# Two sorting networks of a four-layer graph network kernel: VectorE's steps ordered by drains instead of a semaphore

## The chip, the cores and the metric

The kernel runs on one core of a Trainium2 chip. The metric is the device time of one execution in microseconds (us), the median of several runs; less is better.

## What is computed

The reference is four graph layers on 3,125 nodes of 64 features and 53,125 edges (two directions of 25,000 random edges and a loop per node). Each layer normalises the nodes, gathers rows along the edges, reduces them per node and adds the result. Cut to what matters here:

```python
edge_index = jnp.stack([src, dst])
h = relu(layernorm(x)); x = x + L0(h, edge_index, edge_attr_32, ...)     # segment sum, max, mean by src
h = relu(layernorm(x)); x = x + L1(h, edge_index, ...)                   # attention, 8 heads, by dst
h = relu(layernorm(x)); x = x + L2(h, edge_attr_64, ..., src, dst)       # message MLP, mean by dst
h = relu(layernorm(x)); x = x + L3(h, edge_index, edge_weight, ...)      # similarity weights, by src
```

The edges come in an order that depends on the data, so the kernel sorts them on the chip: once by source node and once by destination node. Every gather and every segmented sum runs over these two sorted lists.

## The kernel before

The list of nodes and edges is laid out as 128 partitions x 440 entries (`J`), padded to 128 x 512 for the sorts. Work goes in steps; inside a step the engines run their own programs and meet through semaphores.

- `sort_sources` (lines 284 to 384). VectorE sorts 128 x 512 keys (tiles `sorts_x`) with a bitonic network, in line 334's `sort_network`. Meanwhile TensorE projects the edge attributes (line 595) and ScalarE writes them out as table `recp` (`EdgeTable`, lines 608 to 614), in portions placed between the network's turns (`units_after`). When the sort is done VectorE signals `done_` (line 335). GpSimd waits for it before an iota (line 319); SyncE stores the keys and loads them again in the list's layout, and that load (`keyed`) releases VectorE's line 337 and ScalarE's last portion, and through these `indexed` and `edges_done`, for which GpSimd's gathers wait.
- `layer0_pass` (line 858). GpSimd issues 440 indirect DMAs (line 878), one per list column, back to back, which gather 144 B records into `l0g_rows`. Meanwhile VectorE builds the list data of the first order (`list_setup`), runs the second sort, `sort_destinations` (lines 501 to 554, 128 x 1024 keys, tiles `sortd_x`), builds the second order's data and then sums layer 0 (`layer0_sums`), block by block as the gathered records land.
- After that GpSimd issues further gathers almost without a pause: early edge rows (line 1351), the layer 0 results (line 1008), then `gather_blocks` (line 831) for the layers 1, 2 and 3 and the remaining edge rows (line 1370).

The network has levels k = 1 to 16. A level begins with sign flips of part of the keys (line 437 for k up to 8, lines 441 and 442 for k = 9, line 448 twice for k from 10) and then has k compare steps, b = k-1 down to 0. A compare step is `exchange`: one minimum (line 420) and one maximum (line 421) from one of two buffers into the other. Steps over partitions (b from 9) work on keys that TensorE has transposed: at b = k-1 and at b = 8 of the levels from 10 on, 14 times in all, TensorE turns each of two halves (`turn_blocks`, line 488), ScalarE copies one partner of each pair (`keep_partners`, line 498), and VectorE's exchange reads both, half by half.

Every operation of VectorE in the network adds 1 to the semaphore `step`. VectorE waits for its own count at the start of each level and before every compare step that is not a turn, and at the end; TensorE waits for the count of the half that it turns. Elsewhere in the kernel VectorE orders its own operations with `v.drain()`, without a semaphore.

Of the kernel before, what the change touches and what calls it, by code (L numbers as in the profile page):

```python
# [16 lines left out]
ALU = mybir.AluOpType  # L17
# [266 lines left out]
def sort_sources(K):  # L284
# [4 lines left out]
    with Phase(K, "sorts") as ph:  # L289
# [16 lines left out]
        with Step(nc, pool_ahead=True) as block:  # L306
# [15 lines left out]
            @block.vector  # L322
            def _(dve):
                v = nc.vector
                v.memset(prv[:, :], 0).then_inc(clean, 1)
                dve.wait_ge(consts, 1)
                sort_signs(v, K, bits, sgn, flip, neg)
                dve.wait_ge(loaded, 16)
                v.tensor_scalar(raw[:, :], raw[:, :], 16, None, ALU.logical_shift_left)
                dve.wait_ge(numbered, 1)  # L330
                v.drain()
                v.tensor_tensor(X[0][:, :].bitcast(I32), raw[:, :], K.cid[:, :], ALU.bitwise_or)
                v.drain()
                cur = sort_network(v, dve, X, banks, side, sgn, flip, neg, step, copied, turns)
                v.tensor_scalar(raw[:, :], cur[:, :].bitcast(I32), KEY_ONE - 1, None, ALU.bitwise_and).then_inc(done_, 1)  # L335
                dve.wait_ge(keyed, 16)
                v.tensor_scalar(K.by_src.ent[:, :], key[:, :], 0xFFFF, None, ALU.bitwise_and).then_inc(K.by_src.indexed, 1)
# [62 lines left out]
def halves(x):  # L400

    return x.rearrange("p (q h c) -> p q h c", h=2, c=P)


def partners(x, d):

    if d == 2 * P:
        return x.rearrange("p (l two) (a c) -> p two l a c", two=2, a=1)
    return x.rearrange("p q (a two d) -> p two q a d", two=2, d=d)


def partner_copy(side, s):

    q, a, d = s.shape[2:]
    return side.rearrange("p (q a d) -> p q a d", q=q, a=a)


def exchange(v, out, pair, step):

    v.tensor_tensor(out[0], pair[0], pair[1], ALU.min).then_inc(step, 1)  # L420
    v.tensor_tensor(out[1], pair[0], pair[1], ALU.max).then_inc(step, 1)  # L421


def sort_network(v, dve, X, banks, side, sgn, flip, neg, step, copied, turns):


    n = X[0].shape[1] // SORT_W
    cur, spare = X
    steps = 0
    ready = None  # L430
    for k in range(1, 17):
        dve.wait_ge(step, steps) if steps else None
        if k <= 8:
            half = 2 ** (k - 1)
            w = cur[:, :].rearrange("p (a x) -> p a x", x=4 * half)
            part = w[:, :, 2 * half:] if k == 1 else w[:, :, half:3 * half]
            v.tensor_scalar(part, part, -1.0, None, ALU.mult).then_inc(step, 1)
            steps += 1
        elif k == 9:
            w = cur[:, :].rearrange("p (n x) -> p n x", n=n)  # L440
            v.tensor_scalar(w[:, :, 0:256], w[:, :, 0:256], sgn[:, 0:1], None, ALU.mult).then_inc(step, 1)
            v.tensor_scalar(w[:, :, 256:512], w[:, :, 256:512], neg[:, 0:1], None, ALU.mult).then_inc(step, 1)
            steps += 2
        else:
            ready = []
            for h in range(2):
                part = halves(cur[:, :])[:, :, h]
                v.tensor_scalar(part, part, flip[:, k - 10:k - 9], None, ALU.mult).then_inc(step, 1)
                steps += 1
                ready.append(steps)  # L450
        for b in range(k - 1, -1, -1):
            d = 2 ** (b - 9) if b >= 9 else 2 ** b
            turn = k >= 10 and b in (k - 1, 8)
            if turn:
                turns.append((len(turns), cur, ready, d))
            else:
                dve.wait_ge(step, steps)
            if turn or (k >= 10 and b == 9):
                ready = []
                for h in range(2):  # L460
                    t = partners(halves(spare[:, :])[:, :, h], d)
                    if turn:
                        dve.wait_ge(copied, 2 * len(turns) - 1 + h)
                        s = partners(banks[h].rearrange("p (q c) -> p q c", c=P), d)
                        pair = [s[:, 0], partner_copy(side[:, h], s)]
                    else:
                        s = partners(halves(cur[:, :])[:, :, h], d)
                        pair = [s[:, 0], s[:, 1]]
                    exchange(v, [t[:, 0], t[:, 1]], pair, step)
                    steps += 2  # L470
                    ready.append(steps)
            else:
                s, t = (x[:, :].rearrange("p (a two d) -> p two a d", two=2, d=d) for x in (cur, spare))
                exchange(v, [t[:, 0], t[:, 1]], [s[:, 0], s[:, 1]], step)
                steps += 2
            cur, spare = spare, cur
    dve.wait_ge(step, steps)
    return cur


# [20 lines left out]
def sort_destinations(K):  # L501
# [4 lines left out]
    with Phase(K, "sortd") as ph:  # L506
# [12 lines left out]
        with Step(nc, pool_ahead=True) as block:  # L519
            @block.vector  # L520
            def _(dve):
                v = nc.vector
                sort_signs(v, K, bits, sgn, flip, neg)
                dve.wait_ge(loaded, 48)
                v.tensor_scalar(node[:, 0, :], raw[:, :], 13, None, ALU.logical_shift_left)
                v.tensor_scalar(node[:, 1, :], raw[:, :], 16, None, ALU.logical_shift_left)
                v.tensor_tensor(other[:, 0, :], other[:, 0, :], other[:, 1, :], ALU.bitwise_or)
                v.drain()
                v.tensor_tensor(X[0][:, 0:W].bitcast(I32), node[:, 0, :], other[:, 0, :], ALU.bitwise_or)
                v.tensor_tensor(X[0][:, W:].bitcast(I32), node[:, 1, :], K.cid[:, :], ALU.bitwise_or)  # L530
                v.drain()
                cur = sort_network(v, dve, X, banks, side, sgn, flip, neg, step, copied, turns)
                v.tensor_scalar(node[:, :, :].rearrange("p t w -> p (t w)"), cur[:, :].bitcast(I32), KEY_ONE - 1, None,
                                ALU.bitwise_and).then_inc(done_, 1)
# [2430 lines left out]
```

## Time and profile before

| | us |
|---|---|
| median of 3 runs | 3943.92 (3943.90 to 3944.43) |
| span of the profiled execution | 3095.7 |
| what the median has beside that span | 848.2 |
| VectorE busy | 1326.6 (43%) |
| GpSimd (POOL) busy | 2190.4 (71%) |
| TensorE busy | 610.1 (20%) |
| ScalarE busy | 481.9 (16%) |

The profile gives the span of the profiled execution, from its first to its last instruction, and no other time for that execution; what lies around it is taken as the 848.2 us by which the median is longer. A busy share is an average: here it says little, since nearly all of GpSimd's remaining time is the 0.3 us between two of its indirect DMAs. What must be asked of each stretch is which engine is waited for. The profile also follows back the chain of work that ended last, and tells of each idle time what ended it.

### The profile page before, as it was taken

The page shows a single profiled execution, that of the slowest core. Times are in us where ns is not written, and L with a number is a line of the kernel's source. Part 1 is how long each engine was busy: PE and PEld are TensorE (multiplying, and loading weights), DVE is VectorE, ACT ScalarE, POOL GpSimd, SP SyncE. Part 2 cuts the span into 40 slices and gives each one's busy share as a digit, 9 for nine tenths or more (in the row PEclk, how much of TensorE's full clock was granted, in tenths as well). Part 3 has the DMA queues.
Part 4 walks back from the last instruction along what each step waited for, and adds up shares of the span by engine and source line. Part 5 has one row for each costly group of instructions (what it writes and reads, how often), then busy time and mean ns, then how long its engine had stood idle before and what let it go on. Part 6 is the DMA issues. An engine that isn't in the chain of part 4 may idle for free.

```text
span 3095.7 us, 14532 instructions
## 1 busy us (share of the span) xinstructions
PE 610.1 (20%) x3300; PEld 466.1 (15%) x3301; DVE 1326.6 (43%) x1981; ACT 481.9 (16%) x447; POOL 2190.4 (71%) x2299
## 2 busy tenths in 40 slices
PE   5521130001410000001888860000000400000001
PEld 5411110001300000001676640000000300000001
DVE  8888885202310000008466643233244615353455
ACT  2200006211100000000000022223223212111220
POOL 0177777777777777777777777777777377777774
PEclk8665565555555555555899875555555555555555
DMA  9311114212344755645355424323232123223231
GB/s 325 112 25 14 14 27 100 64 34 63 66 52 53 67 57 60 65 52 65 106 135 155 111 50 74 109 91 128 91 109 92 45 56 85 78 72 91 72 90 52
DMA packets 192274, 248.04 MB, mean 80 GB/s; under 512 B 135507, under 2 KB 146381, under 8 KB 184662
## 3 DMA queue, kind: packets, MB, share of 16 engines
q0 software_dynamic: 74048, 114.24, 19.1%
q1 hardware_dynamic: 60102, 103.67, 10.0%
q10 hardware_dynamic: 58064, 29.51, 7.9%
q14 instruction: 45, 0.37, 0.0%
q8 instruction: 15, 0.25, 0.0%
HBM read 154.17 MB, written 93.09 MB: 80 GB/s over the span
## 4 chain that ended last, share of the span: by engine, by line
POOL 55%; issue 19%; DVE 2%; ACT 0%; DMA 0%; DVEq 0%; POOLq 0%; ACTq 0%
POOL l1g_rows L831 13%; POOL l2g_rows L831 13%; POOL l3g_rows L831 12%; POOL ep_rows L1370 11%; POOL ep_rows L1351 2%; POOL l2t_res L2457 1%; POOL l3t_res L2866 1%; POOL l0f_res L1008 1%; DVE l3g_banks L2813 0%; DVE l3g_banks L2837 0%; ACT l3g_banks L2771 0%; DVE l3g_banks L2834 0%; DVE l3g_dot L2820 0%; DVEq L2819 0%; POOL ep_rows L1379 0%
## 5 line engine op out<-in xcount | busy, mean ns | idle before, releaser
L878 POOL DMA_INDIRECT l0g_rows<-in_rec_s,ents x440 | 427.4, 971 | 137.6 <-issue 133.9
L831 POOL DMA_INDIRECT l2g_rows<-tab,ep_rows x440 | 416.8, 947 | 134.2 <-issue 134.2
L831 POOL DMA_INDIRECT l1g_rows<-tab,srct x440 | 416.8, 947 | 134.2 <-issue 134.2
L831 POOL DMA_INDIRECT l3g_rows<-tab,others x440 | 416.1, 946 | 134.2 <-issue 134.2
L1370 POOL DMA_INDIRECT ep_rows<-recp,entd x352 | 338.7, 962 | 107.3 <-issue 107.3
L1572 DVE TENSOR_TENSOR l1s_A<-l1s_bank,l1s_mk 110x512 f32<-110x512 f32 x8 | 5.2, 686 | 528.4 <-PE l1s_bank L1534 528.4
L1831 PE MATMUL l1a_pa<-l1a_g,l1a_wt 128*128 x1296 | 169.6, 291 | 0.0
L1831 PEld LDWEIGHTS l1a_pa<-l1a_g,l1a_wt 128*128 128x128 f32 x1296 | 158.9, 202 | 23.8 <-issue 23.8
L2811 DVE COPY l3g_banks<-l3g_q 128x65 f32<-128x65 f32 x12 | 2.7, 229 | 306.8 <-ACT l3g_banks L2771 306.4
L2397 DVE COPY l2g_mix<-l2g_q 128x64 f32<-128x64 f32 x11 | 2.5, 228 | 306.9 <-ACT l2g_mix L2358 306.9
L1534 PE MATMUL l1s_bank<-ident,atp 128*110 128x128 f32 x64 | 10.9, 347 | 539.7 <-ACT atp L1473 530.6
L2872 PE MATMUL l3t_nmp<-ident,l3t_nmb 128*64 128x128 f32 x2 | 0.7, 447 | 575.0 <-DVEq L2889 575.0
L1847 DVE TENSOR_TENSOR l1a_wt<-l1a_place,item_ex 128x1536 f32<-128x1536 f32 x54 | 94.9, 1757 | 7.7
L1351 POOL DMA_INDIRECT ep_rows<-recp,entd x82 | 79.1, 964 | 25.0 <-issue 24.7
L319 POOL IOTA iot<- 128x3200 f32 x1 | 2.8, 2803 | 130.0 <-DVE sorts_raw L335 130.0
L1473 ACT COPY atp<-l1g_rows 128x704 f32 (+1 forms) x10 | 8.3, 826 | 552.5 <-DMA l1g_rows<-tab,srct 552.5
L1534 PEld LDWEIGHTS l1s_bank<-ident,atp 128*110 128x110 f32 x64 | 10.4, 217 | 540.4 <-issue 531.1
L2771 ACT COPY l3g_banks<-l3g_rows 128x2860 f32<-128x2860 f32 (+3 forms) x12 | 55.2, 4599 | 220.8 <-DMA l3g_rows<-tab,others 220.7
L420 DVE TENSOR_TENSOR sortd_x<-sortd_x 128x512 f32<-128x512 f32 (+1 forms) x128 | 85.6, 669 | 4.2
L2872 PEld LDWEIGHTS l3t_nmp<-ident,l3t_nmb 128*64 128x64 f32 x2 | 0.3, 203 | 575.2 <-DVEq L2889 575.2
L421 DVE TENSOR_TENSOR sortd_x<-sortd_x 128x512 f32<-128x512 f32 (+1 forms) x128 | 84.5, 660 | 0.0
L2358 ACT COPY l2g_mix<-l2g_rows 128x2816 f32<-128x2816 f32 (+2 forms) x11 | 47.5, 4318 | 231.6 <-DMA l2g_rows<-tab,ep_rows 231.6
(582 smaller groups left out, 2330.2 us busy)
## 6 DMA issues: line engine op xcount, KB each, us to landing
l1a_g<-g SPq DMA_DIRECT2D x54, 390.0 KB
recp<-ep_rows ACTq DMA_DIRECT2D x11, 1320.0 KB, 5.9
g<-l1g_rows ACTq DMA_DIRECT2D x10, 1430.0 KB, 22.7
sums<-l0s_sums SPq DMA_DIRECT2D x10, 1408.0 KB, 5.1
sums<-l2o_sums SPq DMA_DIRECT2D x9, 1408.0 KB, 4.9
sums<-l3o_sums SPq DMA_DIRECT2D x9, 1408.0 KB, 5.3
rowsd<-ep_rows POOLq DMA_DIRECT2D x8, 1452.0 KB, 5.9
ep_rows<-rowsd SPq DMA_DIRECT2D x8, 1452.0 KB, 6.6
```

The lines of the kernel that those rows point to most:

```text
L420: v.tensor_tensor(out[0], pair[0], pair[1], ALU.min).then_inc(step, 1)
L421: v.tensor_tensor(out[1], pair[0], pair[1], ALU.max).then_inc(step, 1)
L831: nc.gpsimd.indirect_dma_start(out=ring.rows[:, s, j, :], out_offset=None, in_=table, in_offset=bass.IndirectOffsetOnAxis(ap=index(b, s, j ...
L878: nc.gpsimd.indirect_dma_start(out=rows[:, j, :], out_offset=None, in_=K.a["rec_s"], in_offset=bass.IndirectOffsetOnAxis(ap=K.by_src.ent[: ...
L1008: nc.gpsimd.indirect_dma_start(out=res[:, w, :], out_offset=None, in_=table, in_offset=bass.IndirectOffsetOnAxis(ap=end[:, w:w + 1], axis= ...
L1351: nc.gpsimd.indirect_dma_start(out=ring.rows[:, s, j, :], out_offset=None, in_=K.recp, in_offset=bass.IndirectOffsetOnAxis(ap=K.by_dst.ent ...
L1370: nc.gpsimd.indirect_dma_start(out=ring.rows[:, s, j, :], out_offset=None, in_=K.recp, in_offset=bass.IndirectOffsetOnAxis(ap=K.by_dst.ent ...
L1831: nc.tensor.matmul(pa[b][:, bass.ds(places[u], P)], wt[:, b, u].rearrange("p h s -> p (h s)"), g[:, b, bass.ds(slots[u], P)], start=False, ...
L1847: v.tensor_tensor(wt[:, b], place[:, b].unsqueeze(2).to_broadcast([P, IB, H, WIN]), K.item_ex[:, :, bass.ds(n * IB, IB)].rearrange("p h i ...
L2358: nc.scalar.copy(cut(bank_of(i), n)[:, :, 1:], ring.rows[:, b % RING, c0:c0 + n, D:].rearrange("p j f -> p f j")).then_inc(spread, 1)
L2457: nc.gpsimd.indirect_dma_start(out=res[:, w, :], out_offset=None, in_=K.sums2, in_offset=bass.IndirectOffsetOnAxis(ap=by.end[:, w:w + 1], ...
L2771: nc.scalar.copy(cut(bank_of(i), C1, n)[:, :, 1:], ring.rows[:, b % RING, c0:c0 + n, C1:].rearrange("p j f -> p f j")).then_inc(spread, 1)
```

## The change

Inside the two sorting networks the operations no longer add to `step`, except the flips of the levels from 10 on and the maximum of the exchanges that work half by half (these are what TensorE turns, or stand beside it). The counts shrink accordingly: one for an exchange instead of two. Where VectorE waited for its own count it now has a drain.

```diff
-def exchange(v, out, pair, step):
-
-    v.tensor_tensor(out[0], pair[0], pair[1], ALU.min).then_inc(step, 1)
-    v.tensor_tensor(out[1], pair[0], pair[1], ALU.max).then_inc(step, 1)
+def exchange(v, out, pair):
+
+    v.tensor_tensor(out[0], pair[0], pair[1], ALU.min)
+    return v.tensor_tensor(out[1], pair[0], pair[1], ALU.max)
...
     for k in range(1, 17):
-        dve.wait_ge(step, steps) if steps else None
+        if k > 1:
+            v.drain()
         if k <= 8:
...
-            v.tensor_scalar(part, part, -1.0, None, ALU.mult).then_inc(step, 1)
-            steps += 1
+            v.tensor_scalar(part, part, -1.0, None, ALU.mult)
         elif k == 9:
...
-            v.tensor_scalar(w[:, :, 0:256], w[:, :, 0:256], sgn[:, 0:1], None, ALU.mult).then_inc(step, 1)
-            v.tensor_scalar(w[:, :, 256:512], w[:, :, 256:512], neg[:, 0:1], None, ALU.mult).then_inc(step, 1)
-            steps += 2
+            v.tensor_scalar(w[:, :, 0:256], w[:, :, 0:256], sgn[:, 0:1], None, ALU.mult)
+            v.tensor_scalar(w[:, :, 256:512], w[:, :, 256:512], neg[:, 0:1], None, ALU.mult)
...
             if turn:
                 turns.append((len(turns), cur, ready, d))
             else:
-                dve.wait_ge(step, steps)
+                v.drain()
...
-                    exchange(v, [t[:, 0], t[:, 1]], pair, step)
-                    steps += 2
+                    exchange(v, [t[:, 0], t[:, 1]], pair).then_inc(step, 1)
+                    steps += 1
                     ready.append(steps)
             else:
...
-                exchange(v, [t[:, 0], t[:, 1]], [s[:, 0], s[:, 1]], step)
-                steps += 2
+                exchange(v, [t[:, 0], t[:, 1]], [s[:, 0], s[:, 1]])
             cur, spare = spare, cur
-    dve.wait_ge(step, steps)
+    v.drain()
     return cur
```

No operation moves to another place or engine. The order of VectorE's instructions at the start of the first network, of the kernel before (a wait stands with the instruction that it holds; drains are not listed):

```order
L437 TENSOR_SCALAR sorts_x<-sorts_x 128x128x2
L420 TENSOR_TENSOR sorts_x<-sorts_x 128x256 [waits sorts_step]
L421 TENSOR_TENSOR sorts_x<-sorts_x 128x256
L437 TENSOR_SCALAR sorts_x<-sorts_x 128x64x4 [waits sorts_step]
L420 TENSOR_TENSOR sorts_x<-sorts_x 128x128x2 [waits sorts_step]
```

And of the changed kernel, at the same place:

```order
L438 TENSOR_SCALAR sorts_x<-sorts_x 128x128x2
L420 TENSOR_TENSOR sorts_x<-sorts_x 128x256
L421 TENSOR_TENSOR sorts_x<-sorts_x 128x256
L438 TENSOR_SCALAR sorts_x<-sorts_x 128x64x4
L420 TENSOR_TENSOR sorts_x<-sorts_x 128x128x2
```

The operations are the same in the same order; only the waits are gone, and drains stand in their places.

## Rows read from the trace of the kernel before

**Rows 1.** The page: engines, GpSimd's 40 slices, and the chain that ended last.
```profile
PE 610.1 (20%) x3300; PEld 466.1 (15%) x3301; DVE 1326.6 (43%) x1981; ACT 481.9 (16%) x447; POOL 2190.4 (71%) x2299
...
POOL 0177777777777777777777777777777377777774
...
POOL 55%; issue 19%; DVE 2%; ACT 0%; DMA 0%; DVEq 0%; POOLq 0%; ACTq 0%
```

**Rows 2.** Who waited for whom, 0 to 140 us: us in total, times, longest.
```profile
POOL iot L319 <- DVE sorts_raw L335: 130.0, 1, 130.0
```

**Rows 3.** Who waited for whom, 140 to 860 us.
```profile
DVE l0s_feats L970 <- ACT l0s_bounds L891: 155.7, 9, 47.8
...
ACT l0s_feats L934 <- DMA l0g_rows<-in_rec_s,ents: 136.2, 3, 46.0
POOL l0g_rows L878 <- issue: 133.9, 439, 0.3
...
POOL l0g_rows L878 <- ACTq L619: 3.7, 1, 3.7
...
POOL rowsd L1332 <- SPq L1314: 3.4, 1, 3.4
```

**Rows 4.** Timeline at the end of the first sort: start, duration, engine, line, operation.
```profile
133.33 0.43 DVE L335 TENSOR_SCALAR sorts_raw<-sorts_x 128x512 int32<-128x512 int32 x1
133.78 0.34 SPq L376 DMA_DIRECT2D keys<-sorts_raw  x1
...
138.34 0.39 DVE L337 TENSOR_SCALAR ents<-first_key 128x440 int32<-128x440 int32 x1 [4.58 <-DMA first_key<-keys]
...
140.34 1.10 POOL L878 DMA_INDIRECT l0g_rows<-in_rec_s,ents  x1 [3.71 <-ACTq L619]
```

**Rows 5.** Groups by form, VectorE, first sort: busy us, mean ns | idle before them.
```profile
L420 DVE TENSOR_TENSOR sorts_x<-sorts_x 128x256 f32<-128x256 f32 x116 | 49.3, 425 | 4.0
...
L420 DVE TENSOR_TENSOR sorts_x<-sorts_turn,sorts_side 128x128 f32<-128x128 f32 x28 | 8.1, 289 | 10.2 <-ACT sorts_side L498 10.2
```

**Rows 6.** Groups by form, VectorE, 470 to 712 us (each of these follows a drain).
```profile
L972 DVE TENSOR_TENSOR_SCAN l0s_totals<-l0s_keeps,l0s_feats 128x1440 f32<-128x1440 f32 x10 | 31.5, 3153 | 0.7
...
L974 DVE COPY l0s_feats<-st 128x32 f32<-128x32 f32 x10 | 1.9, 194 | 0.7
...
L979 DVE COPY st<-l0s_feats 128x32 f32<-128x32 f32 x9 | 1.7, 191 | 0.7
```

**Rows 7.** Timeline of ScalarE, then of VectorE, around the seventh turn (level 13).
```profile
77.82 0.27 ACT L608 COPY ep_rows<-sorts_others 128x40 int32<-128x40 int32 x1 [3.01 <-DMA recp<-ep_rows]
77.95 1.07 ACT L610 COPY ep_rows<-sorts_proj 128x512 f32<-128x512 f32 x2
78.90 0.45 ACT L498 COPY sorts_side<-sorts_turn 128x128 f32<-128x128 f32 x2
...
79.21 0.29 DVE L420 TENSOR_TENSOR sorts_x<-sorts_turn,sorts_side 128x128 f32<-128x128 f32 x1 [1.76 <-ACT sorts_side L498]
```

**Rows 8.** Groups, GpSimd: 195 to 408 us (second sort), then 470 to 700 us.
```profile
L878 POOL DMA_INDIRECT l0g_rows<-in_rec_s,ents x163 | 164.2, 1007 | 49.7 <-issue 49.7
...
L878 POOL DMA_INDIRECT l0g_rows<-in_rec_s,ents x185 | 174.9, 946 | 56.4 <-issue 56.4
```

**Rows 9.** Timeline inside the second sort, VectorE and GpSimd.
```profile
240.49 1.02 POOL L878 DMA_INDIRECT l0g_rows<-in_rec_s,ents  x1 [0.30 <-issue]
240.73 0.69 DVE L420 TENSOR_TENSOR sortd_x<-sortd_x 128x512 f32<-128x512 f32 x1
241.34 0.68 DVE L421 TENSOR_TENSOR sortd_x<-sortd_x 128x512 f32<-128x512 f32 x1
241.82 1.02 POOL L878 DMA_INDIRECT l0g_rows<-in_rec_s,ents  x1 [0.31 <-issue]
242.06 0.69 DVE L420 TENSOR_TENSOR sortd_x<-sortd_x 128x512 f32<-128x512 f32 x1
...
```

**Rows 10.** Timeline of GpSimd over a change of level in the second sort.
```profile
217.09 1.02 POOL L878 DMA_INDIRECT l0g_rows<-in_rec_s,ents  x1 [0.30 <-issue]
218.42 0.95 POOL L878 DMA_INDIRECT l0g_rows<-in_rec_s,ents  x1 [0.31 <-issue]
219.67 0.95 POOL L878 DMA_INDIRECT l0g_rows<-in_rec_s,ents  x1 [0.30 <-issue]
220.92 0.96 POOL L878 DMA_INDIRECT l0g_rows<-in_rec_s,ents  x1 [0.31 <-issue]
222.19 1.03 POOL L878 DMA_INDIRECT l0g_rows<-in_rec_s,ents  x1 [0.30 <-issue]
```

**Rows 11.** The page, groups: an operation of layer 1 that follows a drain.
```profile
L1847 DVE TENSOR_TENSOR l1a_wt<-l1a_place,item_ex 128x1536 f32<-128x1536 f32 x54 | 94.9, 1757 | 7.7
```

## The prediction

> **What bounds the kernel.** I read the page first, then who waits for whom, then the timelines of the places that the change touches. The page [rows 1] shows the chain that ended last as GpSimd's (POOL) issue of gathers, 55%, with another 19% that is the 0.3 us between two of them. Its 40 slices show GpSimd idle in the first slice and the larger part of the second, and busy at a constant seven tenths almost all the way from there. Two questions follow: what does GpSimd wait for at the start, and can anything that VectorE does later slow it?
>
> The waits answer the first: GpSimd waits 130.0 us for the first sort's last operation [rows 2]. The timeline gives the rest [rows 4]: the sort's result is made at 133.33, its keys are stored and loaded again by 138.34, and the first gather starts at 140.34. Nothing else is late there: GpSimd's last wait, 3.7 us on ScalarE's signal [rows 3], is for work that needs the loaded keys too. So the first sort lies wholly on the path. The second sort does not, by its own length: it ends at about 408 us, where the first stretch of [rows 8] is cut, and VectorE afterwards waits 155.7 us in nine pieces for layer 0's blocks, the last one for 47.8 us, because ScalarE waits for gathered records [rows 3]. Only the gathers themselves set the time there, from the first at 140.34 [rows 4] to the last, past 700 us [rows 8].
>
> **The change, part by part.**
>
> *Counts.* In each network a drain replaces a wait on `step` 138 times: levels 1 to 9 have 45 compare steps and 8 level starts with a wait, 53; level k from 10 to 16 has one start and k-2 steps that are no turns, 9+10+...+15 = 84; and one at the end. Removed with them are the increments of all operations outside what is done by halves.
>
> *The increments* I cost at nothing. VectorE starts a maximum before the minimum in front of it has ended, with increments on both (the minimum at 240.73 lasts 0.69, the maximum starts at 241.34 [rows 9]); an increment that held the engine would show there. TensorE waits for the same maximum as before.
>
> *A drain against a wait, inside VectorE.* The 116 full-width minimums of the first sort, which all follow a wait on `step`, have 4.0 us of idle time before them [rows 5], 0.034 us each. Three groups of operations that follow a drain, in code that stays as it is, have 0.7 us before 10, 10 and 9 of them [rows 6], 0.070 to 0.078 each. I take 0.074, the middle, so a drain costs 0.040 us more than the wait that it replaces. From below, the difference could be nothing if much of the 0.034 is not the wait's; from above, the costliest operation behind a drain has 7.7/54 = 0.143 us before it [rows 11], a difference of 0.109. The rows nearest in kind, ordinary operations directly behind a drain, decide for 0.040.
>
> *First sort, on the path:* 138 x 0.040 = 5.5 us. Some of it is taken back where VectorE is not what is waited for. Of the 14 turns, with 10.2 us of waiting in all or 0.73 each [rows 5], the seventh costs 1.76 us instead of the 0.6 to 0.7 of a usual one: ScalarE had first to wait for a DMA that landed at 77.82, and copied the turned half only at 78.90 [rows 7]. VectorE will arrive there 84 x 0.040 = 3.4 us later; if the DMA lands when it did, 1.1 us of waiting vanish. If the landing moves with the sort, nothing vanishes. The queues are full of SyncE's large transfers, which don't depend on VectorE, so I take 1.1. First term: **+4.4 us** (4.2 to 5.5). The later gathers all start that much later, and so does everything behind them.
>
> *Second sort, beside the gathers.* VectorE's own 5.5 us vanish in the 47.8 and 155.7 us above [rows 3]. But the gathers are not independent of it. Away from the sort a gather takes 946 ns and the next starts 0.30 us later, a period of 1.25 us; during the sort the mean is 1007 ns over 163 gathers [rows 8], 61 ns x 163 = 9.9 us lost on the path. The timeline shows how [rows 9]: gathers at 240.49 and 241.82 start 1.33 us apart, and minimums at 240.73 and 242.06 are 1.33 apart too. A gather lasts 1.02 instead of 0.95, as if it needed something that it gets only when an exchange operation ends, and so GpSimd keeps step with the network, one gather to a compare step. A compare step will last 0.040 longer, and a gather in step with it too. I count 94 gathers of 1.01 to 1.03 us in the sort: 94 x 0.040 = 3.8 us. At a change of level the two fall out of step, and three gathers run freely at 0.95 to 0.96 until they are caught again [rows 10]; they slip by 0.078 us (1.328 - 1.250) a gather now and by 0.118 then, so they are caught about one gather sooner, once in each of 15 levels. Such a gather loses the part of a slip that is left, which I put at some 0.07 us: 1.1 us. Second term: **+4.9 us** (0 if they don't stay in step; 5.5, the whole added length of the sort, from above). Below nothing: the bound is the 9.9 us that the sort costs the gathers today.
>
> Here the Trainium skill (SBUF — State Buffer, "SBUF: two separate sides") bears on the rows: VectorE and GpSimd share a pair of ports as an exclusive lock, which an operation with two SBUF inputs holds for its whole length against GpSimd, and the other way round. The first half is what the rows show, a gather that ends later by the rest of an exchange operation. The second half they don't: a minimum lasts 0.69 us with a gather of 1.02 running over it [rows 9], no longer than the first half allows. By the second half, 163 gathers would hold VectorE up to 0.95 us each, some 155 us, as much as its waiting later; I make nothing of it in the sum.
>
> *The sum:* 4.4 + 4.9 = 9.3 us. On the profiled span, 3095.7 becomes 3105.0; what lies around it (848.2 us) has no reason to move, so the median 3943.9 becomes **3953.2**. Downstream nothing takes it back: GpSimd goes on with pauses of 133.9/439 = 0.3 us between its gathers, and its next real wait, 3.4 us [rows 3], ends a chain of layer 0's last sums, which start at the last gather's landing.
>
> **Rivals.**
>
> *Not in step.* The 0.118 us slip lets gathers pass the ends of the exchange operations, or a drain's wider gap serves them as well as today's: the loss stays at 9.9 us and only the first sort counts, 3948.3. For it: a third of the gathers run free even now. Against: each ends up in step within three [rows 10]. 0.21.
>
> *Gathers set free.* One mechanism gives the other side, in the second sort: behind a drain VectorE is idle for 0.074 instead of 0.034 us, and if a gather can take its turn in such a gap without being held to the end of the operation, the 9.9 us go. It decides when the gap is as wide as the gather's need, which must be between 0.034 and the 0.075 by which the gathers are now held. Then 4.4 - 9.9 = -5.5, 3938.4: not slower. Against it: the gather is held *before* the gap, and the gap comes after. 0.09.
>
> *Dearer drains.* At 0.109 us more each, 15.0 us less 1.1 in the first sort and some 94 x 0.109 = 10.2 in the second: 3968. Only one kind of operation shows such a gap [rows 11]. 0.04.
>
> *No difference.* The wait costs as much as a drain, 3943.9. The 0.034 and 0.074 speak against it. 0.04.
>
> *Increments that cost.* If they slow VectorE or the engines waiting in a way that the page doesn't show as idle time, some 0.1 us for each of 138 steps returns, 13.8 - 4.4: 3934.5. The overlap of minimum and maximum speaks against it [rows 9]. 0.07.
>
> **The numbers.** The forecast has 0.55, with a range of its own of 3951.5 to 3956. A measurement of this kernel can tell about 0.2%, 7.9 us, from no change. So slower by more: forecast and dearer drains, 0.59. Faster by more: increments that cost, 0.07. Within: the rest, 0.34. Both sides of that bound hold much, since the forecast lies only 1.4 us beyond it. The range goes from no difference at all to the forecast's upper end, 3943.5 to 3956; outside lie gathers set free, dearer drains and costly increments, 0.20.
>
> **What would show it.** In the changed kernel's profile: idle time before the 116 full-width minimums 8.6 us instead of 4.0; first gather at 144.7 instead of 140.34; compare steps of 1.37 us in the second sort, with gathers 1.37 apart and up to 1.06 long, a mean near 1040 ns; last gather of layer 0 near 710. The wait at the seventh turn falls to 0.6 us. The forecast is wrong in its first term if the first sort ends where it did, and in its second if the mean gather of the second sort stays at or under 1007 ns.

## The result, and the profile after

The changed kernel takes 3952.83 us (median of 17 runs, 3949.55 to 3956.34), the kernel before, run alongside, 3945.53 us (17 runs, 3942.7 to 3949.09). That is 7.3 us more, a ratio of 1.0019 with an interval of 1.0011 to 1.0026. The total of the forecast, +9.3 us, lies inside that interval (4.3 to 10.3 us). How it comes about is another matter.

The page of the changed kernel:

```profile
PE 654.1 (17%) x3300; PEld 480.3 (12%) x3301; DVE 1326.5 (34%) x1981; ACT 481.7 (12%) x447; POOL 2316.4 (59%) x2299
...
POOL 0477777501647777777666300067777735777774
...
POOL 23%; issue 10%; DVE 1%; PE 1%; DVEq 0%; DMA 0%; ACT 0%; POOLq 0%; SPq 0%
```

This is not [rows 1] with something added. Its span is 3954.5 us against 3095.7, its run took 3956.34, and GpSimd, which in [rows 1] is busy at seven tenths from the third slice on, now stands idle in the ninth and tenth slice and for three in the middle. The kernel before, profiled once more, has the same pauses and a span of 3942.1 us (first experiment). **There are two kinds of chip here**: the kernel before takes about 3945 us on the one and about 3097 us on the other. The first profile must have been of the second kind and the times beside it of the first. I call them the 3945 us chips and the 3097 us chips. One chip of the first kind and two of the second were used in the experiments, and each kept its kind in all of its runs; but each was used only once, for four kernels together, so that the kind belongs to the chip, and not to something else that held meanwhile, is not shown. About 1.8 us lie around the span in every run here, not the 848.2 that I took for it. Every ratio below is between kernels on one and the same chip.

**What the forecast said of the first sort shows.** Groups by form, VectorE, first sort of the changed kernel:

```profile
L420 DVE TENSOR_TENSOR sorts_x<-sorts_x 128x256 f32<-128x256 f32 x116 | 49.4, 426 | 9.2 <-issue 0.4
...
L420 DVE TENSOR_TENSOR sorts_x<-sorts_turn,sorts_side 128x128 f32<-128x128 f32 x28 | 8.1, 290 | 12.3 <-ACT sorts_side L496 12.3
```

The 116 minimums have 9.2 us of idle time before them where [rows 5] has 4.0 and I expected 8.6: 0.079 us each, against 0.034. Their duration, 426 ns, has not changed. Over all idle gaps behind the 138 drains of this sort the sum is 10.98 us, against 4.80 in the kernel before on such a chip: 0.045 us a drain, 6.2 in all, where I had 0.040 and 5.5.

The end of the first sort, in the timeline of the changed kernel:

```profile
141.97 0.43 DVE L335 TENSOR_SCALAR sorts_raw<-sorts_x 128x512 int32<-128x512 int32 x1
...
146.96 0.39 DVE L337 TENSOR_SCALAR ents<-first_key 128x440 int32<-128x440 int32 x1 [4.57 <-DMA first_key<-keys]
...
148.96 1.10 POOL L876 DMA_INDIRECT l0g_rows<-in_rec_s,ents  x1 [3.68 <-ACTq L617]
```

The first gather starts at 148.96, not at 144.7: 8.6 us behind [rows 4], and 8.0 behind the kernel before on a chip of this kind (140.94, first experiment). From the sort's result to the gather it is 6.99 us, as in [rows 4] (7.01). So the 8.0 us were added inside the sort, 6.2 of them by drains. The turns have 12.3 us of waiting where [rows 5] has 10.2 and the first experiment 10.6, and the reason is the seventh one (timeline of the changed kernel, ScalarE and VectorE):

```profile
83.99 0.27 ACT L606 COPY ep_rows<-sorts_others 128x40 int32<-128x40 int32 x1 [4.34 <-DMA recp<-ep_rows]
...
85.08 0.45 ACT L496 COPY sorts_side<-sorts_turn 128x128 f32<-128x128 f32 x2
85.39 0.29 DVE L420 TENSOR_TENSOR sorts_x<-sorts_turn,sorts_side 128x128 f32<-128x128 f32 x1 [3.68 <-ACT sorts_side L496]
```

The DMA that ScalarE waits for landed at 83.99, where it landed at 77.82 in [rows 7]. VectorE arrived later and still waited longer, 3.68 us instead of 1.76. Nothing was taken back here. Together with the drains' 6.2 us, the 1.8 us by which the turns wait longer than in the first experiment make up the 8.0.

**What it said of the second sort does not show.** Who waited for whom in the changed kernel, 140 to 1100 us:

```profile
POOL l0f_res L1006 <- DVEq L1025: 184.8, 1, 184.8
...
POOL l0g_rows L876 <- issue: 135.3, 439, 0.9
```

GpSimd is not what sets the time in layer 0. It has done its gathers and then waits 184.8 us for layer 0's sums, which VectorE makes, and VectorE is late because of the second sort. That sort takes 471.2 us (274.5 to 745.7); on a 3097 us chip it takes about 214. The timeline of VectorE and GpSimd inside it:

```profile
281.12 0.95 POOL L876 DMA_INDIRECT l0g_rows<-in_rec_s,ents  x1 [0.30 <-issue]
281.56 0.69 DVE L420 TENSOR_TENSOR sortd_x<-sortd_x 128x512 f32<-128x512 f32 x1 [0.97 <-issue]
282.17 0.69 DVE L421 TENSOR_TENSOR sortd_x<-sortd_x 128x512 f32<-128x512 f32 x1
282.38 1.30 POOL L876 DMA_INDIRECT l0g_rows<-in_rec_s,ents  x1 [0.30 <-issue]
283.98 0.94 POOL L876 DMA_INDIRECT l0g_rows<-in_rec_s,ents  x1 [0.30 <-issue]
284.36 0.69 DVE L420 TENSOR_TENSOR sortd_x<-sortd_x 128x512 f32<-128x512 f32 x1 [1.50 <-issue]
...
287.16 0.43 DVE L438 TENSOR_SCALAR sortd_x<-sortd_x 128x512 f32<-128x512 f32 x1 [1.51 <-issue]
288.56 0.69 DVE L420 TENSOR_TENSOR sortd_x<-sortd_x 128x512 f32<-128x512 f32 x1 [0.97 <-issue]
...
291.36 0.69 DVE L420 TENSOR_TENSOR sortd_x<-sortd_x 128x512 f32<-128x512 f32 x1 [1.50 <-issue]
```

Look at the starts, not the durations. The operations last what they last in [rows 9], 0.69 us, and a maximum follows its minimum as closely. But what stands behind a drain starts at 281.56, 284.36, 287.16, 288.56, 291.36: apart by four, four, two and four times 0.70 us. It looks as if each had to wait for the next mark of a grid, and so a compare step takes 2.1 or 2.8 us instead of the 1.33 of [rows 9]. In the kernel before on such a chip, 82 of the 116 full-width minimums start late, 58 of them by 1.5 us, and all 82 starts lie within 0.04 us on one grid of 0.700 us through the whole sort; the other 34 come in stretches that run as freely as in [rows 9]. At a turn, where TensorE and ScalarE stand between two operations of VectorE, up to 10.4 us are lost. GpSimd is in step here too, with two gathers to a step of 2.80 us, one short and one long (282.38). On such a chip, 0.040 us more behind an operation costs nothing as long as the same mark is met, and 0.70 us where it is missed.

### The profile page after: what moved, and what is told of

It is laid out like the page before. It is cut to its first block and busy times, and to the rows that moved or that the text cites. A ratio compares the mean times of both kernels' runs of the same rounds, so it can differ in the third digit from the quotient of the medians.

```text
span 3954.5 us, 14808 instructions
## 1 busy us (share of the span) xinstructions
PE 654.1 (17%) x3300; PEld 480.3 (12%) x3301; DVE 1326.5 (34%) x1981; ACT 481.7 (12%) x447; POOL 2316.4 (59%) x2299
## 3 DMA queue, kind: packets, MB, share of 16 engines
q0 software_dynamic: 74048, 114.24, 15.6%
## 5 line engine op out<-in xcount | busy, mean ns | idle before, releaser
L876 POOL DMA_INDIRECT l0g_rows<-in_rec_s,ents x440 | 455.3, 1035 | 139.0 <-issue 135.3
L829 POOL DMA_INDIRECT l3g_rows<-tab,others x440 | 449.0, 1021 | 141.2 <-issue 141.2
L829 POOL DMA_INDIRECT l2g_rows<-tab,ep_rows x440 | 445.8, 1013 | 145.3 <-issue 145.3
L829 POOL DMA_INDIRECT l1g_rows<-tab,srct x440 | 450.7, 1024 | 135.2 <-issue 135.2
L1829 PE MATMUL l1a_pa<-l1a_g,l1a_wt 128*128 x1296 | 161.3, 282 | 0.0
L1006 POOL DMA_INDIRECT l0f_res<-sums,ends x25 | 24.2, 967 | 192.1 <-DVEq L1025 184.8
L420 DVE TENSOR_TENSOR sortd_x<-sortd_x 128x512 f32<-128x512 f32 (+1 forms) x128 | 85.5, 668 | 141.2 <-issue 138.6
L1532 PE MATMUL l1s_bank<-ident,atp 128*110 128x128 f32 x64 | 16.2, 427 | 650.0 <-issue 606.1
L486 PE MATMUL sortd_turn<-ident,sortd_x 128*128 128x128 f32 x112 | 29.4, 431 | 429.6 <-issue 353.3
L1773 PE MATMUL l1x_bank<-sel,F 110*128 110x324 f32 x128 | 63.7, 674 | 208.2 <-issue 208.2
L1532 PEld LDWEIGHTS l1s_bank<-ident,atp 128*110 128x110 f32 x64 | 12.3, 217 | 654.0 <-issue 608.3
```

The source lines that it names most:

```text
L829: nc.gpsimd.indirect_dma_start(out=ring.rows[:, s, j, :], out_offset=None, in_=table, in_offset=bass.IndirectOffsetOnAxis(ap=index(b, s, j ...
L876: nc.gpsimd.indirect_dma_start(out=rows[:, j, :], out_offset=None, in_=K.a["rec_s"], in_offset=bass.IndirectOffsetOnAxis(ap=K.by_src.ent[: ...
L1773: lt = nc.tensor.matmul(bank[n % 4][:, 0:HI], K.F[0:CP, h, g * P:(g + 1) * P], K.sel[0:CP, g, i * HI:(i + 1) * HI], start=(g == 0), stop=( ...
L1829: nc.tensor.matmul(pa[b][:, bass.ds(places[u], P)], wt[:, b, u].rearrange("p h s -> p (h s)"), g[:, b, bass.ds(slots[u], P)], start=False, ...
```

## The experiments

Twelve kernels ran, four to a chip. The first four met a 3945 us chip, the other eight two chips of the 3097 us kind.

### The kernel before, once more

No edit.

> The kernel before, unchanged, profiled again. Its first profile has a span of 3095.7 us against a median of 3943.9, while the changed kernel's profile spans 3954.5 against 3956.3. Theory A (the first profile showed an execution that really was faster, or lost 848 us of idle time, and the timed executions are of the other kind): this span is 3940 to 3946, and the second sort takes about as long as the 470 us that it takes in the changed kernel's profile. Theory B (the change itself brought the long waits of the second sort): span and second sort again as in the first profile, 212 us. Time ratio 1.000 in both.

Measured: 3944.73 us (11 runs), ratio 0.9998 (0.9989 to 1.0007), span 3942.1. Who waited for whom, 140 to 1100 us, of this run:

```profile
POOL l0f_res L1008 <- DVEq L1027: 178.8, 1, 178.8
...
POOL l0g_rows L878 <- issue: 135.0, 439, 0.9
```

The long wait for layer 0's sums is there without the change. Where the 846 us between the two profiles of this one kernel lie, by the start of each stage's first gather:

| stage | 3097 us chip | 3945 us chip | later by |
|---|---|---|---|
| layer 0 gathers (L878) | 140.3 | 140.9 | 0.6 |
| layer 0 results (L1008) | 729.5 | 955.0 | 225.5 |
| layer 1 gathers (L831) | 841.6 | 1125.1 | 283.5 |
| layer 2 gathers (L831) | 1852.8 | 2568.1 | 715.3 |
| layer 3 gathers (L831) | 2483.6 | 3277.8 | 794.2 |
| end of span | 3095.7 | 3942.1 | 846.4 |

Until the gathers begin the chips are alike; then each layer takes longer. The grid is there while GpSimd gathers, and not otherwise. Its last gather before a pause starts at 775.23, and VectorE's timeline behind it reads:

```profile
786.20 0.16 DVE L743 TENSOR_TENSOR nmd<-afterd,setd_c 128x1 f32<-128x1 f32 x1 [0.71 <-issue]
786.90 0.16 DVE L749 TENSOR_TENSOR setd_c<-nmd,setd_c 128x1 f32<-128x1 f32 x1 [0.54 <-issue]
787.60 0.15 DVE L751 TENSOR_SCALAR setd_c<-setd_c 128x1 f32<-128x1 f32 x1 [0.55 <-issue]
787.67 0.15 DVE L752 TENSOR_SCALAR setd_c<-setd_node 128x1 f32<-128x1 f32 x1
788.31 0.16 DVE L754 TENSOR_TENSOR setd_c<-setd_c,afterd 128x1 f32<-128x1 f32 x1 [0.50 <-issue]
788.54 0.16 DVE L756 TENSOR_TENSOR setd_c<-setd_c 128x1 f32<-128x1 f32 x1
```

786.20, 786.90, 787.60 are marks; from 788.3 on operations of the same kind follow each other freely, some 12 us after the last gather started. So the marks go on for a while when no gather is issued any more, at an interval that is not the 1.25 us of free gathers. What makes the grid I don't know.

### Drains in the first sort alone

In the changed kernel, the second sort gets the old network back (a copy of it, with its increments and waits):

```
@@ sort_destinations
-                cur = sort_network(v, dve, X, banks, side, sgn, flip, neg, step, copied, turns)
+                cur = sort_network_signalled(v, dve, X, banks, side, sgn, flip, neg, step, copied, turns)
```

> Drains in the first sort only; the second sort keeps waits on the semaphore. Prediction's first term: +5 to +8 us over before (the first sort has become 8 us longer in the changed kernel's profile), and nothing more. If the loss of 7.3 us were made in the second sort: 0.

Measured: 3954.15 us (10 runs) against 3945.89 before on this chip, +8.3 us, ratio 1.0021 (1.0012 to 1.0031). Its first sort ends at 141.06, that of the kernel before at 134.33; the second lasts 469.0 us as before (469.1). What is lost in the first sort, 6.7 us by its end, is still there at the end of the kernel, as far as the interval (4.7 to 12.2 us) can tell.

### Drains in the second sort alone

The same edit in sort_sources instead.

> Drains in the second sort only. Prediction's second term (gathers in step with longer compare steps): +4.9 us over before. If the second sort has waits much longer than a drain, as the changed kernel's profile shows, they hide the 40 ns and the loss is 0; if drains there catch fewer or more of these waits, it may have either sign, up to 10 us.

Measured: 3949.57 us (11 runs), +3.7 us, ratio 1.0009 (1.0000 to 1.0018): at the edge of what can be told from nothing. The first sort ends at 135.60. The second takes 471.2 us, as in the changed kernel, 2.1 more than in the kernel before: three marks of the grid. The two groups in which it is decided show how little those 2.1 us say about a drain. Of the kernel before on this chip, by form, VectorE, 271 to 741 us:

```profile
L420 DVE TENSOR_TENSOR sortd_x<-sortd_x 128x512 f32<-128x512 f32 x116 | 80.8, 697 | 121.3 <-DVE sortd_x L421 80.5 <-issue 19.1 <-remote 15.3
...
L420 DVE TENSOR_TENSOR sortd_x<-sortd_turn,sortd_side 128x256 f32<-128x256 f32 x28 | 11.9, 425 | 127.4 <-issue 124.6 <-ACT sortd_side L498 2.7
```

Of the changed kernel, 274 to 746 us:

```profile
L420 DVE TENSOR_TENSOR sortd_x<-sortd_x 128x512 f32<-128x512 f32 x116 | 80.4, 693 | 135.0 <-issue 132.4
...
L420 DVE TENSOR_TENSOR sortd_x<-sortd_turn,sortd_side 128x256 f32<-128x256 f32 x28 | 11.9, 425 | 115.0 <-issue 103.5 <-ACT sortd_side L496 11.1
```

The steps at full width lose 13.7 us more before their minimums, some twenty marks missed, and the turns lose 12.4 us less. A likely reading, not tried by itself, is that a step that ends late leaves less to wait for at the next meeting with TensorE and ScalarE.

### Each drain twice

```
@@ sort_network, at its three drains
     v.drain()
+    v.drain()
```

> The changed kernel with two drains in place of each one, in both sorts. If a drain costs 40 to 70 ns on the first sort's path: 138 more of them give +5 to +10 us over the changed kernel, so +13 to +18 over before. If a second drain behind a first is free (the engine is already empty), +7 as the changed kernel.

Measured: 3955.95 us (7 runs), +10.1 us over the kernel before, ratio 1.0029 (1.0018 to 1.0041). In its first sort, by form:

```profile
L420 DVE TENSOR_TENSOR sorts_x<-sorts_x 128x256 f32<-128x256 f32 x116 | 49.4, 426 | 15.9 <-issue 1.8
```

0.137 us each, against 0.079 with one drain and 0.034 with a wait. So the price grows with the drains and is theirs, and a second drain, behind which nothing should be left to wait for, still costs 0.058 us: a drain has a price of its own even there. Over its 138 places the second drains add 7.9 us to the first sort, but it ends at 147.68, only 5.3 us later than in the changed kernel. The other 2.7 us are taken back at the turns, which wait 9.7 us in all instead of 12.3: when VectorE comes to the seventh, the store has landed, and it waits 0.77 us instead of 3.68. The second sort is as long as with one drain (471.3 us). The whole is 10.1 us over the kernel before where +13 to +18 was expected; its interval (7.1 to 16.2 us) and that of the changed kernel (4.3 to 10.3) are too wide to tell whether the 5.3 us are all still there at the end.

### Gathers held until the second sort has ended

A wait ahead of GpSimd's 440 gathers, in the kernel before and in the changed one, so that the sort runs without them:

```
+                v.sem_inc(K.sorted2, 1)              # sort_sources, behind the last operation
...
                 for j in range(J):
+                    if j == 0:
+                        pool.wait_ge(K.sorted2, 1)
```

> The kernel before, but GpSimd issues the 440 gathers of layer 0 only after the second sort. Theory T (the gathers hold up VectorE's steps in the second sort, which makes it take 469 us): the sort then takes about 212 us, as in the first profile, with 34 ns before a minimum; the layer's sums wait for the gathers instead, so the whole is 0 to 80 us slower than before. Rival (the waits of the second sort are its own, whatever GpSimd does): the sort still takes 469 us and the kernel becomes over 400 us slower.

> The changed kernel with the same hold. Against the held kernel before: with theory T both sorts lie on the path undisturbed, so 138 drains more at 0.045 us count twice, +12 to +15 us; the second sort goes from about 212 to 218 us. If drains cost nothing in the second sort even then: +7.

Measured, on a 3097 us chip: 3353.05 us before and 3363.29 after (5 runs each), ratios to the kernel before as it is, 3097.09 us, of 1.0821 (1.0806 to 1.0836) and 1.0856 (1.0841 to 1.0871). By form, VectorE, in the second sort, with the drains out (190 to 405 us):

```profile
L420 DVE TENSOR_TENSOR sortd_x<-sortd_x 128x512 f32<-128x512 f32 x116 | 80.3, 692 | 4.0
```

and with them (196 to 417 us):

```profile
L420 DVE TENSOR_TENSOR sortd_x<-sortd_x 128x512 f32<-128x512 f32 x116 | 80.3, 693 | 9.2 <-issue 0.4
```

With nothing of GpSimd beside it the second sort shows the first one's numbers again, 4.0 and 9.2, at twice the width: the gap behind a drain is the same at both. The sort is 6.1 us longer (219.5 against 213.4), the first gather 12.1 us later (415.8 against 403.7), and the total 10.2, a little under the +12 to +15 expected and within the noise of the two ratios: with the sort uncovered, both sorts' drains are on the path. In the first sort of this pair the turns do take something back, 0.9 us in all, the seventh waiting 0.57 us instead of 1.26. Holding the gathers costs 256 us by itself; the 0 to 80 expected were reckoned for a 3945 us chip.

Held gathers last 948 ns on average in both kernels, against the 1007 of [rows 8]. So the sort is what lengthens them. Whether holding them takes the grid away on a 3945 us chip was the question I most wanted answered; the run met the other kind, and it stays open.

### No increment on the minimums

In the kernel before, half of the increments of an exchange go:

```
-    v.tensor_tensor(out[0], pair[0], pair[1], ALU.min).then_inc(step, 1)
+    v.tensor_tensor(out[0], pair[0], pair[1], ALU.min)
...
-                steps += 2
+                steps += 1
```

> The kernel before with its waits kept, but only the maximum of an exchange adds to the semaphore, not the minimum (264+28 increments fewer in all, no drain). If increments cost nothing: ratio 1.000, and 34 ns before a minimum as before. If they cost (the rival of the prediction): 5 us or more faster.

Measured: 3098.62 us (11 runs), ratio 1.0003 (0.9994 to 1.0012). By form, first sort:

```profile
L420 DVE TENSOR_TENSOR sorts_x<-sorts_x 128x256 f32<-128x256 f32 x116 | 49.3, 425 | 4.0
```

The same 4.0 us as in [rows 5]. The increment on a minimum costs nothing that can be measured (the rival needed 9.4 us from all increments; of the half removed here not even 2 us are within the interval), and so the change had nothing to win: the rival "increments that cost" is out, if the increment on a maximum, which stayed here, costs no more. The Trainium skill says this as well (VectorE: DVE Perf Modes, "The DRAIN you can't avoid"): a semaphore after each of eight copies made them no longer than one after the last. By that rule, too, there was nothing to win; the run agrees, with 1.0003.

### SyncE's zero stores later

In the changed kernel, the four stores of zeros into `tab2` and `tab3n`, three of 800 KB and one of 12.5 KB, go from the start of the step to its end, just ahead of the wait for them:

```
-                sp.dma_start(node_rows(K.tab2[0:NP, D:]), K.hn[:, :, :]).then_inc(zeroed, 16)
...
                 sp.wait_ge(done_, 1)
...
+                sp.dma_start(node_rows(K.tab2[0:NP, D:]), K.hn[:, :, :]).then_inc(zeroed, 16)
...
                 sp.wait_ge(zeroed, 64)
```

> The changed kernel with SyncE's four stores of zeros (lines 370 to 374) moved behind the loads of the sorted keys, out of the first sort. If the long wait at the seventh turn (3.7 us in the changed kernel's profile, 1.8 before, 0.8 with double drains) comes from these stores: it falls to 0.57 to 0.68, and the first sort ends 3 us earlier, at about 139.3. The whole: 0 to 3 us faster than the changed kernel. If it comes from ScalarE's own copies, the wait stays.

Measured: 3109.96 us (5 runs), ratio 1.0039 (1.0025 to 1.0052). Timeline at the seventh turn:

```profile
81.99 0.29 DVE L420 TENSOR_TENSOR sorts_x<-sorts_turn,sorts_side 128x128 f32<-128x128 f32 x1 [0.57 <-ACT sorts_side L496]
```

The wait is that of any other turn. In each of the thirteen other profiles ScalarE waits there for its DMA, 0.80 to 4.62 us, as in [rows 7]; here that wait is gone. The DMA issues give size and time to landing of the store that it waits for, first of the kernel before, then of the changed one, then of this run:

```profile
recp<-ep_rows ACTq DMA_DIRECT2D x1, 1320.0 KB, 13.2
...
recp<-ep_rows ACTq DMA_DIRECT2D x1, 1320.0 KB, 16.3
...
recp<-ep_rows ACTq DMA_DIRECT2D x1, 1320.0 KB, 4.5
```

So the store of records lands late because of the zeros in flight on the other queue; it is one run, but in the thirteen others the same store takes 12.3 to 16.3 us. They show one thing more. The landing is at 77.6 to 79.8 us in the seven kernels without drains in the first sort, and at 79.9 to 84.0 in the six with them, 4.2 us later on average. ScalarE issues this store between two turns of the network, and so it goes out later too: at 64.2 to 65.5 us without drains, at 66.9 to 70.1 with them. The time to landing varies by 4 us beside. VectorE's wait at this turn is 0.57 to 3.68 us, without an order: 1.76 and 1.88 for the kernel before, 3.68 and 2.08 for the changed one. The first sort ends at 139.01, 1.8 us sooner than in the changed kernel on a chip of this kind (140.81), and the last gather starts 1.3 us sooner (711.8 against 713.1), though the zeros, now behind the first sort, go with a second sort that starts at 225.4 us instead of 201.1; the gathers cover that. In the total nothing of it is seen, with 1.0039 here and 1.0037 there.

### The changed kernel on a 3097 us chip

No edit. These three runs, the changed kernel and its two halves, are the test of the forecast on the chip from whose profile it was made.

> The changed kernel once more, beside the kernel before. The kernel before takes about 3945 us on one chip and about 3097 on another. If this chip is of the first kind: +7 us again, second sort about 470 us. If of the second kind (that of the first profile): the first sort ends at 139 to 142, the mean gather inside the second sort is 1040 ns, the last gather of layer 0 ends near 713, and the whole is +9 to +13 us. The rival that the gathers do not stay in step: mean gather 1007 ns or less, +5 to +7.

Measured: 3107.61 us (5 runs) against 3097.73, +9.9 us, ratio 1.0037 (1.0023 to 1.0051). The group of gathers in the second sort, 201 to 421 us:

```profile
L876 POOL DMA_INDIRECT l0g_rows<-in_rec_s,ents x164 | 171.0, 1043 | 50.0 <-issue 50.0
```

1043 ns where [rows 8] has 1007. The timeline of both engines inside it:

```profile
238.50 1.06 POOL L876 DMA_INDIRECT l0g_rows<-in_rec_s,ents  x1 [0.30 <-issue]
238.82 0.69 DVE L420 TENSOR_TENSOR sortd_x<-sortd_x 128x512 f32<-128x512 f32 x1
...
239.87 1.05 POOL L876 DMA_INDIRECT l0g_rows<-in_rec_s,ents  x1 [0.30 <-issue]
240.19 0.69 DVE L420 TENSOR_TENSOR sortd_x<-sortd_x 128x512 f32<-128x512 f32 x1
...
241.23 1.07 POOL L876 DMA_INDIRECT l0g_rows<-in_rec_s,ents  x1 [0.30 <-issue]
241.55 0.69 DVE L420 TENSOR_TENSOR sortd_x<-sortd_x 128x512 f32<-128x512 f32 x1
```

Minimums 1.37 and 1.36 us apart, gathers 1.37 and 1.36 apart, a gather 1.05 to 1.07 long: in step, one gather to a compare step, as [rows 9] and 0.040 us more. 91 gathers last between 1.055 and 1.072 us, where I had counted on 94. Over the sort the gathers lose 15.6 us (164 x 0.095) instead of 9.9.

### The two halves on a 3097 us chip

The edits of "first sort alone" and "second sort alone" again.

> Drains in the first sort only. Chip of the first kind: +6 to +8 as before. Of the second kind: +5 to +7, gathers in the second sort at a mean of 1007 ns, 9 to 11 us lost as in the first profile.

> Drains in the second sort only. Chip of the first kind: +2 to +4. Of the second kind, theory of the gathers in step: +5 us though VectorE's own 5.5 us are hidden, with a mean gather of 1040 ns inside the sort. Rival (only what VectorE itself does late counts, and it is hidden): 0.

Measured: first sort alone 3105.58 us (11 runs), +7.9, ratio 1.0028 (1.0019 to 1.0037); second alone 3102.41 us (11 runs), +4.7, ratio 1.0017 (1.0008 to 1.0026). The gathers in the second sort, with drains in the first sort alone (202 to 416 us):

```profile
L939 POOL DMA_INDIRECT l0g_rows<-in_rec_s,ents x164 | 165.1, 1007 | 50.0 <-issue 50.0
```

and with drains in the second alone (195 to 414 us):

```profile
L939 POOL DMA_INDIRECT l0g_rows<-in_rec_s,ents x163 | 169.6, 1040 | 49.7 <-issue 49.7
```

The lengthening of the gathers, 5.4 us (163 x 0.033), belongs to the second sort's drains and to nothing else: the four kernels of this kind without drains there that keep the gathers beside it have means of 1007 to 1015 ns. The total, +4.7 us with an interval of 2.5 to 8.1, fits it, though VectorE's own delay is hidden there.

### A pause ahead of the last gathers

The kernel before, with the wait of the held gathers only at `j == (NBLK - 2) * TB`, near the end of the 440. On a 3945 us chip the second sort is still running there, and without gathers its rest might leave the grid: a version that could beat both kernels.

> The kernel before, but the last 88 of layer 0's 440 gathers wait for the second sort. Chip of the first kind (gathers hold up VectorE in the second sort, and GpSimd then waits 179 us for the layer's sums): the sort gets free sooner, 10 to 45 us faster. Of the second kind: the 352nd gather ends at about 590, long after the sort, so the wait never holds, and the time is the same.

Measured: 3097.77 us (11 runs), ratio 1.0002 (0.9993 to 1.0012). It met a 3097 us chip, where the sort has long ended and the wait never holds, so it says nothing of the idea. It does show how much the seventh turn varies without any drain: 3.25 us here, 1.76 in [rows 7]. No kernel of the twelve beats the kernel before.

## Why the prediction was right, and where it was not

**"What lies around it (848.2 us) has no reason to move".** This step failed first. I set a span of 3095.7 beside a median of 3943.9 and took the difference for something around the execution. It was a profile of the other kind of chip: 1.8 us lie around the span (3956.34 against 3954.5), and the 846 us lie inside it, from the first gathers on. A gap of a fifth between a span and its time was the most striking number that I had, and I explained it in half a sentence.

**"Only the gathers themselves set the time there".** True of the profile that I read and not of the chips that were timed. There VectorE's second sort ends at 740 us instead of 408, and GpSimd waits 178.8 us for the sums behind it.

**A drain costs 0.040 us more than the wait.** Right, and a little short: 0.045 over the 138, 6.2 us where I had 5.5. The choice by the nearest rows, [rows 6], held; the 0.109 of [rows 11] was no drain's price.

**"1.1 us of waiting vanish" at the seventh turn.** Failed. I had named the alternative, that the landing moves with the sort, and chose against it because the transfers in front don't depend on VectorE. They don't, but the store that ScalarE waits for is its own, issued between two turns. In the kernel before and in the changed one:

```profile
64.59 0.33 ACTq L614 DMA_DIRECT2D recp<-ep_rows  x1
...
67.64 0.33 ACTq L612 DMA_DIRECT2D recp<-ep_rows  x1
```

The landing came 4.2 us later on average with drains in the first sort, and it varies by as much from run to run, which one profile can't show. So the wait can grow or go: it went with the gathers held (1.26 to 0.57 us) and with double drains (0.77), and grew in the changed kernel (3.68).

**First term, +4.4.** Too low: +8.3 us on the one kind of chip (ratio 1.0012 to 1.0031, so 4.7 to 12.2 us) and +7.9 on the other (5.9 to 11.5). 6.2 of it are the drains; the other 2 us are within these intervals, and in the changed kernel's own profile 1.8 are its longer wait at the seventh turn, which the other profiles don't tie to drains.

**Second term, +4.9, gathers in step with the network.** Right in mechanism and in size where the gathers set the time: +4.7 us, mean 1040 to 1043 ns for "near 1040", steps of 1.37. The rival "not in step" is out there, and "gathers set free" too. On the 3945 us chips the term has no ground: the mean gather in the sort is 1062 ns in the kernel before and 1060 in the changed one, and GpSimd waits for the sums afterwards anyway. What stands in its place is 2.1 us of marks missed in the sort itself, in a total that is 3.7 us longer (0 to 7.1).

**The rule on the shared ports** (the Trainium skill, SBUF — State Buffer, "SBUF: two separate sides"). The trace agrees with its first half: gathers of 948 ns alone last 1.01 to 1.07 us, until 0.05 to 0.09 us behind the end of a two-input operation. The second half, GpSimd holding the pair for its whole instruction, does not show on the 3097 us chips: a minimum lasts 0.69 us under a gather that started before it, as it does with the gathers held. On the 3945 us chips it stays open. There too a minimum lasts 0.69 us, the waits come before operations, and the marks go on 0.70 us apart some 10 us after the last gather; but within the sort the two engines are in step, two gathers to a step of 2.80 us, so that a lock has no part in these waits is not shown.

**The sum.** +9.3 us forecast, +7.3 measured, and +9.9 on the chips of the first profile. On those the forecast would have stood for its reasons, if the first term's miss is left aside. On the chips that gave the median, 7.3 agrees with the halves, 8.3 and 3.7, within their intervals, and with my sum by luck: two steps wrong in opposite ways, a first term too small and a second whose mechanism isn't at work there.

**"Slower by over 0.2%", 0.59.** The measured 0.19% lies just inside that bound, on the side to which I gave 0.34, with an interval that reaches from 0.11 to 0.26%; on the chips of the first profile it is 0.37%, beyond the bound. That the forecast sat on the bound was said; it sits there still.

## What to carry to other kernels

Ordering an engine's own steps by an explicit drain instead of a wait on its own semaphore costs some 0.045 us a step here and saves nothing that the runs show; do it for simplicity, not for time. Before anything is built on a profile, set its span beside the time of that same execution: 1.8 us lay between them here, and 848 meant that the profile was of another kind of chip than the times, with another engine as the bound in layer 0. And work that is hidden can still cost: on the 3097 us chips the second sort's drains lay wholly beside GpSimd's gathers and made 163 of them 0.033 us longer on average. Last, ask of a transfer that an engine waits for not only what is in front of it but who issues it, and whether that moves.

## What the runs showed of the hardware that I had not expected

- **Two kinds of chip for one kernel**: 3945 and 3097 us, a ratio of 1.27, the same up to the first gather (140.9 and 140.3 us). Why is open.
- **A grid of 0.70 us.** On the 3945 us chips, while GpSimd issues gathers, most operations of VectorE behind a wait or a drain (82 of 116 minimums) start on marks 0.70 us apart, mostly 1.5 us late, at a turn up to 10.4. The second sort takes 469 us instead of 214, with the same 116 minimums of 0.69 us in it. The cause is open, and whether holding the gathers removes it wasn't tried on such a chip.
- **A second drain in a row costs 0.058 us**, no less than one drain costs over a wait (0.045): 0.034, 0.079 and 0.137 us before a minimum behind a wait, one drain and two.
- **A store is held up by stores on another engine's queue**: ScalarE's 1320 KB land 12.3 to 16.3 us after their issue while SyncE's zeros (three times 800 KB) are in flight, by an amount that changes from run to run, and 4.5 us after it with the zeros moved.
